# Tridiagonal reduction in a graph network: work of a wide column moved between engines, and one more filler matmul with four tiles

## The reference

```
deg = sum(A, 0) + sum(A, 1) - diag(A)
L_norm = d_inv_sqrt[:, None] * (diag(deg) - A) * d_inv_sqrt[None, :]
_, U = eigh(L_norm)
h = relu(einsum(U.T, features) @ W1 + b1)
x = layernorm(x + einsum(U, h @ W2 + b2))
```

## Time and profile before

| | us |
|---|---|
| median of 3 runs | 4421.01 |
| lowest, highest | 4419.71, 4425.44 |
| profiled execution, its own time | 4428.78 |
| its span, first to last instruction | 4427.0 |
| mean granted TensorE clock | 0.594 of full |
| PE, PEld busy | 3284.3 (74%), 2507.4 (57%) |
| DVE, POOL, ACT busy | 2720.7 (61%), 1620.1 (37%), 954.8 (22%) |

### The profile page before, as it was taken

The page is one execution under the profiler, slowest core; times in us unless marked ns, Lnnn a source line. Parts: engine busy times, 40 slices in busy tenths (PEclk is TensorE's granted clock), DMA queues, the critical chain, the costliest instruction groups (busy, mean ns, idle before and its releaser), DMA issues.

```text
span 4427.0 us, 79301 instructions
## 1 busy us (share of the span) xinstructions
PE 3284.3 (74%) x21761; PEld 2507.4 (57%) x21761; DVE 2720.7 (61%) x15582; ACT 954.8 (22%) x4267; POOL 1620.1 (37%) x7282
## 2 busy tenths in 40 slices
PE   7999999999999999998898887777511324221068
PEld 7677787777767776766777776666411322110034
DVE  4445444454444444455545556777888999999934
ACT  2222222222222222222222223444200001000013
POOL 5564444444445544555555554444200000000000
PEclk6656556665555555566666665555555666565589
DMA  2000000000000000000000000000000000000001
GB/s 54 2 2 2 2 2 2 2 2 1 1 1 1 1 1 1 2 1 5 1 1 1 1 1 1 1 1 1 27 1 0 1 0 0 0 0 0 0 0 39
DMA packets 14656, 18.51 MB, mean 4 GB/s; under 512 B 1665, under 2 KB 11009, under 8 KB 13953
## 3 DMA queue, kind: packets, MB, share of 16 engines
q1 hardware_dynamic: 14208, 13.42, 1.0%
HBM read 9.22 MB, written 4.19 MB: 3 GB/s over the span
## 4 chain that ended last, share of the span: by engine, by line
PE 54%; DVE 32%; POOL 6%; issue 5%; ACT 3%; DVEq 0%; DMA 0%; POOLq 0%; ACTq 0%
PE ps L762 10%; PE ps L723 7%; PE ps L696 5%; PE ps L688 5%; PE ps L674 4%; PE ps L742 4%; DVE h L2254 4%; PE ps L749 3%; PE ps L831 2%; PE ps L820 2%; DVE ps L1673 2%; DVE small L1662 1%; PE ps L818 1%; PE ps L1033 1%; ACT small L1376 1%
## 5 line engine op out<-in xcount | busy, mean ns | idle before, releaser
L762 PEld LDWEIGHTS ps<-UR 128*128 128x128 f32 x2552 | 540.4, 290 | 331.9 <-DVE UR L1757 176.5
L762 PE MATMUL ps<-UR 128*128 128x41 f32 (+19 forms) x2552 | 530.1, 353 | 137.4 <-ACT UR L1412 69.0
L1667 DVE RECIPROCAL small<-small 128x1 f32<-128x1 f32 x511 | 83.7, 164 | 707.2 <-ACT small L1376 703.4
L1146 POOL TENSOR_SCALAR small<-small 128x1 f32<-128x1 f32 x511 | 118.2, 231 | 894.5 <-ACT small L1378 889.4
L1750 DVE SCALAR_TENSOR_TENSOR small<-small,ps 128x1 f32<-128x1 f32 x383 | 84.4, 220 | 523.3 <-PE ps L831 522.9
L742 PE MATMUL ps<-UR,ident 128*128 128x18 f32 (+2 forms) x1020 | 297.8, 381 | 116.2 <-DVE UR L1675 108.5
L749 PEld LDWEIGHTS ps<-cw,big 128*128 128x128 bf16 x11088 | 377.1, 106 | 11.0 <-POOL cw L1144 6.4
L723 PE MATMUL ps<-ident 128*128 128x256 f32 x860 | 381.4, 589 | 0.5 <-ACT h L1319 0.5
L749 PE MATMUL ps<-cw,big 128*128 128x3 bf16 x11088 | 345.1, 166 | 10.0 <-POOL cw L1144 5.8
L831 PEld LDWEIGHTS ps<-small,ones 128*128 128x128 f32 x766 | 200.8, 299 | 229.1 <-issue 118.0
L742 PEld LDWEIGHTS ps<-UR,ident 128*128 128x128 f32 x1020 | 236.6, 288 | 149.6 <-DVE UR L1675 135.3
(11 more groups left out here) (623 smaller groups left out, 7905.1 us busy)
## 6 DMA issues: line engine op xcount, KB each, us to landing
out<-xs SPq DMA_DIRECT2D x16, 256.0 KB, 2.3
m<-in_adj SPq DMA_DIRECT2D x1, 1024.0 KB, 5.2
before<-c_before SPq DMA_DIRECT2D x1, 1024.0 KB, 5.3
notafter<-c_notafter SPq DMA_DIRECT2D x1, 1024.0 KB, 7.4
sib<-c_sib SPq DMA_DIRECT2D x1, 448.0 KB, 3.2
own<-c_own SPq DMA_DIRECT2D x1, 384.0 KB, 3.1
big<-c_iota SPq DMA_DIRECT2D x1, 256.0 KB, 3.6
h<-c_lanes SPq DMA_DIRECT2D x1, 186.0 KB, 3.2
```

What stands on the lines that cost most here:

```text
L762: last = nc.tensor.matmul(ps[2][:, 0:2 * npend + 3], over(x_of(j)), flat[:, j, 2 * first:2 * k + 3], start=(j == tp), stop=(j == T - 1))
```

## The change

In wide columns: GpSimd makes x times mask (`xm2`) right behind the split of x, and VectorE's `uc2` is gone. The factor 1/q comes in through L831, whose weights are now `RQ` spread over a square instead of ones, so that `RQ` is made ahead of y and not behind it. `own_column` stands ahead of `TMP` and x, no longer behind x. `GZ` no longer waits for `SG`, and `HAL` stands behind `P0`; VectorE's `Q` waits for both. The two pivot entries of `tcol2` are made by ScalarE ahead of `yq`, no longer by GpSimd, which makes `BETAQ` ahead of the unit entry, and the unit entry in one instruction less. In the fillers: columns with four tiles get one more identity matmul at place 2 (`extra`), in another PSUM bank, and the first eight columns three a place instead of two. The narrow columns keep their work; only the numbers that they wait for follow.

```diff
         sparks = sb("sparks", [P, P, 2])
+        minus_sparks = sb("minus_sparks", [P, P])
...
         signs_ready = sem("signs_ready")
+        xm_ready = sem("xm_ready")
+        mb_ready = sem("mb_ready")
...
         xsp16 = cw[:, 0:12].bitcast(BF16).rearrange("p (t c h) -> p t c h", c=3, h=2)
-        pair_masks, uc2, tcol2 = (cw[:, 12 + 8 * i:20 + 8 * i].rearrange("p (t s) -> p t s", s=2) for i in range(3))
+        pair_masks, xm2, tcol2 = (cw[:, 12 + 8 * i:20 + 8 * i].rearrange("p (t s) -> p t s", s=2) for i in range(3))
...
             wanted = (0, 1, 1) if n_on > 1 else (0, 0, 0)
-            extra = (0, 0, 0)
+            extra = (0, 0, 1) if n_on > 3 else (0, 0, 0)
             if k < 8:
-                wanted, extra = (0, 0, 0), (0, 2, 2)
+                wanted, extra = (0, 0, 0), (0, 3, 3)
...
-                if halves_of[k][place] and k >= 8 and not counted["closed"]:
+                if place == 1 and halves_of[k][place] and k >= 8 and not counted["closed"]:
...
                 for _ in range(halves_of[k][place]):
-                    nc.tensor.matmul(ps[6][:, 0:2 * P].rearrange("p (a d) -> p a d", a=2), ident[:, 0:P],
+                    nc.tensor.matmul(ps[6 if place == 1 else 2][:, 2 * P:4 * P].rearrange("p (a d) -> p a d", a=2), ident[:, 0:P],
...
                 if n_on > 1:
+                    pe.wait_ge(rq_ready, k + 1)
                     pe.wait_ge(y_ready, k + 1)
-                    nc.tensor.matmul(ps[3][:, 8:10], ones[:, :], CY, start=True, stop=True).then_inc(cy_ready, 1)
+                    nc.tensor.matmul(ps[3][:, 8:10], over(RQ), CY, start=True, stop=True).then_inc(cy_ready, 1)
...
             nc.gpsimd.tensor_copy(ident16, ident[:, 0:P])
+            ts(minus_sparks[:, :], ident[:, 0:P], -SPARK, None, ALU.mult)
...
                 tp, n_on, pp = window_of(k)
-                z(tt(U1, AL, erow[:, k:k + 1], ALU.subtract))
-                z(tt(U1, U1, GT, ALU.mult))
+                z(ts(U1, AL, erow[:, k:k + 1], GT, ALU.subtract, ALU.mult))
...
                     tt(xsp[:, on, 2], xsp[:, on, 1], xsp16[:, on, 1, 1], ALU.subtract).then_inc(split_ready, 1)
+                    pool.wait_ge(masks_ready, k + 1)
+                    tt(xm2[:, 0:n_on, :], pairs[:, on, k, 1:2].broadcast_to([P, n_on, 2]), pair_masks[:, on, :], ALU.mult).then_inc(xm_ready, 1)
                 pool.wait_ge(root_ready, 2 * k + 2)
-                z(ts(SG, AL, 0.0, 0.5, ALU.is_ge, ALU.subtract))
-                tt(HAL, AL, SG, ALU.mult).then_inc(signs_ready, 1)
+                z.post(ts(SG, AL, 0.0, 0.5, ALU.is_ge, ALU.subtract))
...
                 tt(P0, GZ, SG, ALU.mult).then_inc(signs_ready, 1)
+                tt(HAL, AL, SG, ALU.mult).then_inc(signs_ready, 1)
...
                     pool.wait_ge(masks_ready, k + 1)
-                    z(ts(MBS, pair_masks[:, tp + special, :], NINVB, None, ALU.mult))
-                    pool.wait_ge(y_done, k + 1)
-                    ts(tcol2[:, special, 0:1], MBS[:, 0:1], y[:, special:special + 1], None, ALU.mult)
-                    ts(tcol2[:, special, 1:2], MBS[:, 1:2], y[:, special:special + 1], sparks[:, (k + 2) % P, 1:2],
-                       ALU.mult, ALU.subtract).then_inc(pivot_t_ready, 1)
+                    ts(MBS, pair_masks[:, tp + special, :], NINVB, None, ALU.mult).then_inc(mb_ready, 1)
+                    pool.wait_ge(rq_ready, k + 1)
                     pool.wait_ge(beta_ready, k + 1)
+                    tt(BETAQ, erow[:, k:k + 1], RQ, ALU.mult).then_inc(bq_ready, 1)
                     unit_added(k)
-                    pool.wait_ge(rq_ready, k + 1)
-                    tt(BETAQ, erow[:, k:k + 1], RQ, ALU.mult).then_inc(bq_ready, 1)
                     if k + 1 < narrow_from:
-                        pool.wait_ge(ucn_ready, k + 1)
+                        pool.wait_ge(xm_ready, k + 1)
+                        pool.wait_ge(mb_ready, k + 1)
...
                                                  ACT.Copy, scale=NINVB).then_inc(t_ready, 1)
+                        act.wait_ge(mb_ready, k + 1)
+                        nc.scalar.activation(tcol2[:, special, 0:1], y[:, special:special + 1], ACT.Copy, scale=MBS[:, 0:1])
+                        nc.scalar.activation(tcol2[:, special, 1:2], y[:, special:special + 1], ACT.Identity, scale=MBS[:, 1:2],
+                                             bias=minus_sparks[:, after:after + 1]).then_inc(pivot_t_ready, 1)
...
                         act.wait_ge(u1_ready, k + 1 - narrow_from)
-                        act.wait_ge(ucn_ready, k + 1)
+                        act.wait_ge(ucn_ready, k + 1 - narrow_from)
...
                 has_rb = h_.mark(nc.vector.reciprocal(RB, RN))
-                dve.wait_ge(signs_ready, 3 * k + 1)
+                dve.wait_ge(signs_ready, 3 * k + 2)
...
                 h_.wait(has_rb)
-                dve.wait_ge(signs_ready, 3 * k + 2)
                 stt(out=NINVB, in0=P0, scalar=-8.0, in1=RB, op0=ALU.mult, op1=ALU.mult).then_inc(invb_ready, 1)
+                h_.wait(has_q)
+                nc.vector.reciprocal(RQ, Q).then_inc(rq_ready, 1)
...
                 summed(y[:, here], n_on, npend, am[:, 0:216]).then_inc(y_done, 1)
-                h_.wait(has_q)
-                nc.vector.reciprocal(RQ, Q).then_inc(rq_ready, 1)
...
                     op0=ALU.mult, op1=ALU.mult, accum_out=CY[:, 0:1]).then_inc(y_ready, 1)
-                dve.wait_ge(rq_ready, k + 1)
-                dve.wait_ge(masks_ready, k + 1)
-                stt(out=uc2[:, here, :], in0=pairs[:, on, k, 1:2].broadcast_to([P, n_on, 2]), scalar=RQ, in1=pair_masks[:, on, :],
-                    op0=ALU.mult, op1=ALU.mult).then_inc(ucn_ready, 1)
...
                     dve.wait_ge(pivot_row_ready, k)
-                    has_column = products(on, n_on, first, npend, ps[4], am[:, 216:432])
+                    h_.wait(products(on, n_on, first, npend, ps[4], am[:, 216:432]))
+                h_.post(own_column(k))
...
                 h_.wait(has_tmp)
-                dve.wait_ge(ucn_ready, k + 1)
+                dve.wait_ge(xm_ready, k + 1)
...
                 off = on_next.start - tp
-                stt(out=pairs[:, on_next, k + 1, :], in0=uc2[:, off:n_on, :], scalar=TMP, in1=tcol2[:, off:n_on, :],
+                stt(out=pairs[:, on_next, k + 1, :], in0=xm2[:, off:n_on, :], scalar=TMP, in1=tcol2[:, off:n_on, :],
                     op0=ALU.mult, op1=ALU.subtract).then_inc(x_ready, 1)
-                if npend:
-                    h_.wait(has_column)
-                h_(own_column(k))
...
                 has_rb = h_.mark(nc.vector.reciprocal(RB, RN))
-                dve.wait_ge(signs_ready, 3 * k + 1)
+                dve.wait_ge(signs_ready, 3 * k + 2)
...
                 h_.wait(has_tmp)
-                dve.wait_ge(ucn_ready, k + 1)
+                dve.wait_ge(ucn_ready, k + 1 - narrow_from)
...
```

## The result

The changed kernel takes 4284.7 us (median of 4 runs, 4254.22 to 4316.74) against 4421.89: the ratio is 0.969, with a 95% interval of 0.9612 to 0.9768. Its four runs lie 1.5% apart, the four of before 0.13%. The profiled execution has a span of 4297.5 us.

What follows compares the result with a forecast made beforehand. TensorE was taken to bound most wide columns, GpSimd those behind fast stretches. Terms of -22 (two tiles), -6 (three) and +1 (four) gave -27 us: 4402 in the profiled execution, 4394 as median; range 4330 to 4458.

Steps and rivals of the forecast that it cites:

- the latency gain: Two- and three-tile columns: shorter waits for GpSimd let L762 start earlier; 22 and 6 us less.
- The stream: Four-tile columns: the added identity matmul costs time, but the clock gives most back; net 1 us more.
- the columns with 512-wide fillers: Four tiles, 54 columns: a fast stretch expected behind every one, 6.85 us each, 0.2 less than now; 11 us less.
- The short matmuls: Four tiles, eight columns at clock 0.50: no answer of the clock, full 0.97 us each; 8 us more.
- the second case: Rival: with four tiles the clock goes up and stays up, 4313 us; chance 0.13.
- the third: Rival: with four tiles the stream is paid and the clock doesn't answer, 4471 us; chance 0.25.
- the forecast case: All wide columns: latency gains with the stream about even, -27 us, reaching -9 to -50 (4371 to 4412); chance 0.45.
- the two sentences on when the clock rises and falls: TensorE's clock, from the Trainium skill: activity releases the throttle; a pause in every turn of a loop throttles again.
- `RQ` ahead of y: Wide columns: paid by `NINVB` with two tiles; with three, y 0.11 us later in some 20 columns, 2 us.
- The pivot entries and BETAQ: Two tiles: pivot operations leave GpSimd, `BETAQ` moves ahead; L1166 ends well over a microsecond earlier, its wait gone.
- the two marks of being wrong: Mean clock with four tiles: staying near 0.61 (slower) or above 0.75 (much faster) would refute the forecast of about 0.68.
- My rival of a gain taken up by the fillers: Two tiles: a shorter way to L762 shifts the fast stretch where it is worth less; 4416 us, chance 0.17.

Runs made afterwards that it cites:

- bare: The kernel before, or the changed kernel, without any identity matmul: 550.8 and 497.6 us for the last 99 two-tile columns (283 to 381).
- the last version: Changed kernel without the added streams, with weights of ones (`RQ` behind y) and without any identity matmul: 4192.82 us, ratio 0.9479.

## Why the prediction was wrong

**The step that failed** is the size of the latency gain: 17 us in 99 two-tile columns, "for all 127 columns 17 x 127/99 = 22 us less. Bounds: 0 [...] and 27, all of it", and 6 us with three tiles. They measured 105 and 57. I read the idle time that the profile showed before L762, 16.3 us, as all that could be had. It was a sum over the few columns at the upper clock, and I left the number of these columns as it was.

**What the runs showed in its place** are two things. The bare way through a two-tile column became 0.54 us shorter in the mean, 53 us in the 99, three times the idle time that the earlier trace rows had for it. And with fillers the 99 gained 90.6 us. The columns sorted by their granted clock say how. A column at 0.50 throughout takes 6.47 us in both kernels (medians of the 46 and 33 such columns): there the fillers cover the shorter way in full. A column at 1.00 takes 4.35 instead of 4.89, and there were 6 of these before, never two in a row, and 40 after, up to 8 in a row. So much of the gain comes from columns that moved to the upper clock: it is 0.75 in the mean instead of 0.64. With three tiles it is the same picture: 6.90 us at 0.50 in both kernels, 102 such columns before and 83 after. Undoing the row sum shows the factor too, 33.4 us bare, and with fillers 582.63 against 521.84, 61 us:

```profile
2043.06:2625.69 582.63, 527.76 (x3057) 426.28 (x3056) 296.04 (x2104) 190.73 (x927) 295.45 (x1385) 0.67 0.01 2
```

The factor is not a rule, though. The row sum and `BETAQ` in the kernel before gave 28.3 us bare and 22.3 with fillers (590.07), and the row sum alone 4.7 bare and 9.0 more, not less, with fillers. That a shorter way keeps the clock up, by fillers that stand closer together, is argued from these rows; no run here sets the clock by itself, and each of them is of one execution.

**The stream** was forecast at net 1 us with bounds of -15 to +10. The run of it alone has 15 as a whole [4 to 27], and in the profiles of the changed kernel with and without it four tiles differ by 36.8. The mechanism stood: the clock went up, to 0.66 where I had said 0.68, and paid part of the price. The term that was too good is the columns with 512-wide fillers. I had expected 6.85 us instead of 7.06; the 29 of the earlier trace rows take 7.22 with the stream alone and 7.27 in the changed kernel. The short matmuls cost nearly the full length, as said, 0.85 and 0.93 us a column at 0.50. Neither the second case nor the third came.

**Sums and readings.** By the stated bounds of the terms, 0 to -36 for latency and -15 to +10 for the stream, the forecast case would reach from -51 to +10 us; the -9 at which it ends is where a gain can be told, and no bound of a term. And 0.97 and 0.53 us, weighted four to one by the clock of 0.61, give 0.88 us a column and 105 in all, not 0.78 and 93. Neither moves the forecast of -27. The rows named for the two sentences on when the clock rises and falls fit them, but show less: PE is busy for 37.52 of 37.88 us at 0.50 and for 19.66 of 20.37 us at 1.00, so its busy time in the profile doesn't tell the two apart, and in the earlier trace rows the clock rises, 0.50 to 0.79, without a pause of PE in either column.

**`RQ` ahead of y** I had called paid by `NINVB` with two tiles. It wasn't: weights of ones save 0.13 us a bare column there, and `NINVB` came no earlier, 1.42 us behind L1379 as against 1.43 behind L1376.

**The pivot entries and BETAQ** went as said: no wait for GpSimd is left at L1651 or at x in the changed kernel. Either of the two is enough to have `BETAQ` in time. But `BETAQ` ahead of the unit entry makes the unit entry late, and the pivot entries have to leave GpSimd for that one's sake, a wait that the prediction didn't have.

**Hidden work.** The row sum beside L831 costs nothing that a run shows with two tiles, and what follows the wide columns is the same to 3 us.

**Signs that misled.** Of what the profile was to show, the waits for GpSimd gone, L762's idle for L1644 under 4 us and 238 more L723 all came true, and four tiles at 0.66 lay between the two marks of being wrong. These signs were of the mechanism that I had; the size of the gain was not in them.

My rival of a gain taken up by the fillers was the wrong way round for the whole change, and right in the 99 for the row sum alone. I had the two-way traffic between a column's length and its clock in the text for four tiles, and gave a gain by it no chance where the column itself gets shorter.

## What to carry to other kernels

Where fillers cover a dependency chain and the granted clock moves between two levels, the idle time in the profile doesn't bound what a shorter chain brings: here 16 us of idle time stood against 91 us in the same columns, and one shortening, the row sum alone, gave nothing there with its fillers in. Take the fillers out once, in both versions, and compare the bare chains; then time the whole with its fillers. If an instruction waits for several producers, price them together, and ask what the reordering makes late: here it was the unit entry. A filler that is there for the clock must be timed against none at all: here the identity matmuls, taken together, cost about 1% more than they gave.

## What the runs showed of the hardware

With the same instructions a two-tile column took 6.47 us at a granted clock of 0.50 and about 4.35 at 1.00 in the changed kernel, and the clock changed between the two 32 times in the 99 (49 times in the kernel before).

Executions of one program differ by as much as some parts of the change are worth: 4254 to 4317 us for the changed kernel, 4211.9 to 4278.6 for the one without the stream, 4416 to 4460 for the kernel before beside the last three runs, and 4190.31 to 4195.17 for the last version, which has 99 columns without fillers. Whether the time at the upper clock makes the scatter is not shown, since the kernel before lay within 0.13% once and 1.0% another time. Between two executions of one program the four-tile stretch alone differed by some 18 us: 881.8 in the single one with weights of ones and no identity matmuls, and 899.7 in the profile of its later runs, on another chip. The 99 agreed better, 484.96 and 485.42 in these two, and 612.40 and 612.41 in the kernel before without and with the stream. With fillers and a clock that changes they don't: 521.84 and 487.07 for the same code. A difference of ten us in one such stretch of one profile is weak evidence.
